# Attention scores as one fp16 product of 96 stacked rows per head, with query and key halves carried through DRAM, and the stages from the scores on one iteration later

## What is computed

```
x = x + tanh(g_xattn) * attention(layernorm(x), ctx, ctx)      # B=2, S=2048, E=512, T=128 keys, 16 heads of 32
    q = (query @ Wq.T + bq), k = (key @ Wk.T + bk), v = (value @ Wv.T + bv)   split into heads
    att = q k^T / sqrt(32); masked by pad_mask and subsq_mask; prob = softmax(att); out = prob v
x = x + tanh(g_ffn) * ffn(layernorm(x))
    shared_out = (silu(x sg) * (x su)) sd
    top 2 of softmax(x router), 8 experts: routed = sum of coef * ((silu(x gate) * (x up)) down)
```

## Time and profile before

| | us |
|---|---|
| median of 3 runs | 1158.11 (1152.9 to 1160.1) |
| the profiled execution, its own time | 1157.58 |
| its span in the trace | 1155.8 |
| pass 1 up to the end of iteration 12 on DVE | 180.71 |
| iterations 13 to 31 (19 iterations) | 270.04 |

### The profile page before, as it was taken

The page is one execution under the profiler, slowest core; times in us unless marked ns, Lnnn a source line. Parts: engine busy times, 40 slices in busy tenths (PEclk is TensorE's granted clock), DMA queues, the critical chain, the costliest instruction groups (busy, mean ns, idle before and its releaser), DMA issues.

```text
span 1155.8 us, 26617 instructions
## 1 busy us (share of the span) xinstructions
PE 1050.2 (91%) x7344; PEld 677.3 (59%) x7345; DVE 822.7 (71%) x2938; ACT 531.4 (46%) x1041; POOL 441.8 (38%) x654
## 2 busy tenths in 40 slices
PE   4699979999999999860899999999999999999997
PEld 3488767777777777660455555555554444444443
DVE  5899868788888888763576666666665666666666
ACT  1366546666666666640444444444443232232322
POOL 3254647676667667442112112112110423232322
PEclk9999889999999999855899999999999999999999
DMA  7555573223323223432233333333332544444543
GB/s 290 197 177 179 131 173 95 93 93 93 93 93 94 94 93 110 101 102 72 74 110 118 115 113 118 118 109 118 118 109 67 185 158 161 157 168 149 169 149 128
DMA packets 76731, 146.96 MB, mean 127 GB/s; under 512 B 20912, under 2 KB 23088, under 8 KB 73872
## 3 DMA queue, kind: packets, MB, share of 16 engines
q1 hardware_dynamic: 46512, 66.01, 20.0%
q10 hardware_dynamic: 17280, 44.83, 10.5%
q0 software_dynamic: 12896, 35.58, 9.9%
HBM read 94.04 MB, written 52.35 MB: 127 GB/s over the span
## 4 chain that ended last, share of the span: by engine, by line
PE 64%; issue 11%; DVE 9%; POOL 8%; ACT 4%; DMA 2%; POOLq 1%; another core or an unknown queue 1%; SPq 0%; DVEq 0%; ACTq 0%
PE bank L1046 15%; PE bank L1047 15%; PE bank L1048 15%; PE bank L1038 8%; PE bank L1090 3%; PE bank L1108 3%; DVE arena L776 3%; POOL arena L467 3%; POOL token_of_row L503 2%; ACT arena L605 1%; DVE arena L865 1%; POOL arena L474 1%; DMA token_of_row<-arena 1%; DVE peak L879 1%; PE bank L1064 1%
## 5 line engine op out<-in xcount | busy, mean ns | idle before, releaser
L1046 PE MATMUL bank<-weights,arena 128*128 (+1 forms) x682 | 259.9, 381 | 2.1 <-ACT arena L647 1.9
L1047 PE MATMUL bank<-weights,arena 128*128 (+1 forms) x682 | 259.8, 381 | 0.0
L1048 PE MATMUL bank<-weights,arena 128*128 (+1 forms) x682 | 259.6, 381 | 0.0
L1038 PE MATMUL bank<-ident,arena 128*128 128x128 f32 (+1 forms) x1592 | 189.4, 267 | 56.1 <-DMA arena<-normed_rows,arena 25.7
L1038 PEld LDWEIGHTS bank<-ident,arena 128*128 128x128 f32 (+1 forms) x1592 | 161.4, 132 | 103.0 <-issue 71.9
L514 POOL DMA_INDIRECT arena<-normed_rows,arena x71 | 67.1, 946 | 254.9 <-PE bank L1038 238.7
L1108 PEld LDWEIGHTS bank<-arena 128*128 128x128 f32 x1024 | 131.7, 198 | 34.3 <-issue 29.5
L1090 PE MATMUL bank<-arena 128*128 128x512 f32 x256 | 138.8, 647 | 5.4 <-DVE arena L776 5.1
L1108 PE MATMUL bank<-arena 128*128 128x33 f32 x1024 | 128.8, 276 | 2.9 <-issue 1.8
L467 POOL TENSOR_TENSOR arena<-arena 128x512 f32<-128x512 f32 x96 | 101.3, 1056 | 76.8 <-DVE arena L776 75.7
L524 POOL DMA_INDIRECT arena<-expert_rows,arena x64 | 62.8, 981 | 173.9 <-DVE arena L998 156.1
(11 more groups left out here) (175 smaller groups left out, 1895.7 us busy)
## 6 DMA issues: line engine op xcount, KB each, us to landing
expert_rows<-arena ACTq DMA_DIRECT2D x71, 256.0 KB, 2.1
arena<-in_x SPq DMA_DIRECT2D x64, 256.0 KB, 3.2
weights<-in_w_gu ACTq DMA_DIRECT2D x8, 1024.0 KB, 4.7
x_rows<-arena SPq DMA_DIRECT2D x32, 256.0 KB
normed_rows<-arena SPq DMA_DIRECT2D x32, 256.0 KB, 4.9
normed_transposed<-arena SPq DMA_DIRECT2D x32, 256.0 KB, 2.3
arena<-normed_transposed SPq DMA_DIRECT2D x32, 256.0 KB, 3.3
arena<-x_rows SPq DMA_DIRECT2D x32, 256.0 KB, 3.4
```

The lines of the kernel that those rows point to most:

```text
L1038: last = t.transpose(dst[:, c * P:(c + 1) * P], src[:, c * P:(c + 1) * P], (ident16 if src.dtype == F16 else ident)[:, :])
L1046: t.matmul(dst, hi[:, rows], w_hi(c), start=(c == 0), stop=False)
L1047: t.matmul(dst, hi[:, rows], w_lo(c), start=False, stop=False)
L1048: last = t.matmul(dst, lo[:, rows], w_hi(c), start=False, stop=(c == chunks - 1))
```

## The change

1. The scores. Before, one fp32 product per group of four heads: 128 rows of `q_t` by 128x512 of `kbd`. Now, q is scaled, split in two fp16 halves and stacked on 96 partitions per head (upper, lower, upper), against keys stacked (upper, lower, upper of the array `k_halves`), so that one fp16 product of 96 rows by 128 columns gives a head's scores; four such products per group (`scores(k)`, L1144 of the new kernel).
2. The halves are moved across partitions through DRAM: SP writes `q_halves` to `q_dram` (one DMA), waits for its landing, and reads it back into `q_stack` in three DMAs of 32 partitions each (`stack`). The keys go the same way once (`k_dram`).
3. The copy of the queries out of `bank[0]`: ACT's four pieces of `q_t` become one fp16 copy at the end of its body (q_hi), and DVE gets a new step at the start of its next body, the lower half (q_lo). The query bias is now one more small product of PE per 128 columns (L1179 of the new kernel, `bq_half` and `bias_row`); the scale of the scores is applied by ACT's exponential.
4. The scores and all behind them have a lag one higher: LAG1 is 9, and there are 41 iterations.
5. PE's transposition of the normalised tile, first in its body before, stands behind `mix_values(0)`. ACT's x_hi, first in its body before, stands behind `exponent(0)`. DVE's x_lo, before `maxima(0)` until now, stands behind `maxima(1)`.
6. SP's body has a new order, with the q write first and the stack loads behind the loads of x.
7. Before the first scores: the peak of the keys and a scale for them (a third use of the peaks' transposition, `turn_peaks(7, 2)`), and three steps of POOL for the bias; the `memset` of `kbd` and the sixteen writes into it are gone. In passes 2 and 3 several semaphores are merged into one that counts on; their steps and their order are the same.

```diff
-        LAG1, LAG2, LAG3, SPAN2 = 8, 4, 4, 4
+        LAG1, LAG2, LAG3, SPAN2 = 9, 4, 4, 4
...
 SP body
+                n, j, u = tile(J, v, 3)
+                if live(n, NT):
+                    hold(sp, sp_passed, (q_ready, n + 1))
+                    sp.dma_start(q_dram[u].rearrange("a p n -> p a n"), q_halves.rearrange("p (a n) -> p a n", a=2)).then_inc(q_out[u], 16)
...
+                    hold(sp, sp_passed, (q_out[u], 16 * (j + 1)))
+                    hold(sp, sp_passed, (s_done, group(n - 2, EC - 1)))
+                    stack(q_stack[u], q_dram[u], q_stacked[u])
...
+            def stack(dst, src, done):
+
+                for at, part in enumerate((0, 1, 0)):
+                    sp.dma_start(dst[at * D:(at + 1) * D, :].rearrange("d (h n) -> d h n", h=HG),
+                                 src[part].rearrange("(h d) n -> d h n", h=HG)).then_inc(done, 16)
...
 ACT body
-                    act.wait_ge(xt_done, n + 1)
-                    need(act, q_done, n)
-                    a.activation(x_hi, bank[0][:, :], ACT.Copy, scale=X_SCALE).then_inc(hi_ready, 1)
...
                 take_probs(0)
                 take_probs(1)
                 exponent(0)
+                n, j, u = tile(J, v, 2)
+                if live(n, NT):
+                    act.wait_ge(xt_done, n + 1)
+                    need(act, q_done, n)
+                    a.activation(x_hi, bank[0][:, :], ACT.Copy, scale=X_SCALE).then_inc(hi_ready, 1)
...
-                    for c in range(EC):
-                        last = a.activation(q_t[u][:, c * P:(c + 1) * P], bank[0][:, c * P:(c + 1) * P], ACT.Identity,
-                                            scale=w_back[:, 0:1], bias=bq_s[:, c:c + 1])
-                    last.then_inc(q_ready, 1)
+                    hold(act, act_passed, (q_out[(v - 3) % 2], 16 * (j + u)))
+                    a.activation(q_halves[:, 0:E], bank[0][:, :], ACT.Copy, scale=Q_DOWN).then_inc(q_hi_ready, 1)
...
 DVE body
+                n, j, u = tile(J, v, 3)
+                if live(n, NT):
+                    dve.wait_ge(q_hi_ready, n + 1)
+                    d.scalar_tensor_tensor(q_halves[:, E:2 * E], bank[0][:, :], Q_DOWN, q_halves[:, 0:E], ALU.mult, ALU.subtract).then_inc(q_ready, 1)
...
-                n, j, u = tile(J, v, 2)
-                if live(n, NT):
-                    dve.wait_ge(hi_ready, n + 1)
-                    d.scalar_tensor_tensor(x_lo, bank[0][:, :], X_SCALE, x_hi, ALU.mult, ALU.subtract).then_inc(lo_ready, 1)
                 maxima(0)
...
                 maxima(1)
-                normalise(1, 5)
+                n, j, u = tile(J, v, 2)
+                if live(n, NT):
+                    dve.wait_ge(hi_ready, n + 1)
+                    d.scalar_tensor_tensor(x_lo, bank[0][:, :], X_SCALE, x_hi, ALU.mult, ALU.subtract).then_inc(lo_ready, 1)
+                normalise(1, 6)
...
 PE body
-                    transposes(bank[0], xn[u], EC).then_inc(xt_done, 1)
-
                 def scores(k):
-                    n, j, u = tile(J, v, 3)
+                    n, j, u = tile(J, v, 4)
                     if live(n, NT):
-                        pe.wait_ge(q_ready, n + 1)
+                        pe.wait_ge(q_stacked[u], 16 * PARTS * (j + 1))
+                        pe.wait_ge(k_stacked, 16 * PARTS)
                         need(pe, max_done, group(n, k - 2))
-                        t.matmul(bank[2 + k % 2][:, :], q_t[u][:, k * P:(k + 1) * P], kbd[:, u, k, :],
-                                 start=True, stop=True).then_inc(s_done, 1)
+                        for h in range(HG):
+                            q_at, k_at = (h * EC + k) * P, ((h * EC + k) * B + u) * T
+                            last = t.matmul(bank[2 + k % 2][:, h * T:(h + 1) * T], q_stack[u][0:STACK, q_at:q_at + P],
+                                            k_stack[0:STACK, k_at:k_at + T], start=True, stop=True)
+                        last.then_inc(s_done, 1)
...
+                            last = t.matmul(dst, bq_half[:, co * P:(co + 1) * P], bias_row[:, :], start=False, stop=True)
...
                 mix_values(0)
+                n, j, u = tile(J, v, 2)
+                if live(n, NT):
+                    pe.wait_ge(xn_ready, n + 1)
+                    need(pe, q_ready, n)
+                    transposes(bank[0], xn[u], EC).then_inc(xt_done, 1)
                 scores(2)
```

More of the change, by code:

```diff
@@ L150, in build @@
         x_hi, x_lo = carve(E // 2).bitcast(F16), carve(E // 2).bitcast(F16)
-        q_t = [carve(E) for _ in range(2)]
+        q_halves = carve(E).bitcast(F16)
+        q_stack = [carve(H * T // 2).bitcast(F16) for _ in range(2)]
         attn = carve(E)
@@ L597, in body @@
                         sc = score[u][:, h * T:(h + 1) * T]
-                        last = a.activation(sc, sc, ACT.Exp, bias=peaks_neg[:, h - H + HG:h - H + HG + 1])
+                        last = a.activation(sc, sc, ACT.Exp, scale=score_scale[:, :], bias=peaks_neg[:, h - H + HG:h - H + HG + 1])
                     last.then_inc(exp_done, 1)
```

292 lines of the change are left out of this document (166 added, 126 removed).

## The result

The changed kernel takes 1229.35 us, the median of 4 runs (1226.53 to 1233.14), against 1159.11 us (1152.9 to 1162.04, 4 runs): a ratio of 1.0617, interval 1.0578 to 1.0656. The direction and the mechanism were forecast, the size was not: 1199 was said, and 1226 was the end of the range. The profiled execution took 1233.14 us, its span 1231.3, which is 75.5 more than before.

A forecast was written before the change was run, and what follows sets the result against it. Pass 1 was taken to stand on two close limits, PE and a ring through POOL. Terms 20.8 + 10 + 7 + 3 = 41 us on 1157.6 gave 1198.4, about 1199 against the median; range 1162 to 1226.

The forecast's parts named there:

- What bounds the kernel now: Pass 1, 14.21 us per iteration: odd iterations set by PE and mendable, even ones by a 14.3 us loop through POOL.
- The moved x_hi and x_lo: Steady iterations 13 to 31: DVE's second half waits for POOL and ACT, 16.2 us even, 14.5 odd, +20.8 us.
- PE's work: Pass 1 scores: PE's iteration falls from 12.7 to about 10.0 us, but this brings no gain since PE waits.
- The start: Before the first scores: PE's first transposition waits for a longer chain of peaks and DVE steps, +3 us (1 to 5).
- The q path through DRAM: SP's query write and three reads per iteration: about 10 us at most, hidden within 14 us, so 0 us.
- One more iteration: Pass 1 runs 41 iterations instead of 40: +10 us, between about 9 and 14.5.
- the other iterations with scores: About ten iterations before 12 and in the drain: 0 to 1.5 us each, 0.7 taken, +7 us.
- The signs: Expected in the loop's profile: L881 idle about 3 us each, shift(0) never idle before, scores near 1 us, PE at most 75%.
- The waits did not vanish: Rival for the loop: POOL's stretch from L873 to shift(0) shrinks, so DVE's waits vanish; 1137 to 1152 us, chance 0.16.
- Start and drain were not free: Rival: the steady loop loses as forecast, but start and drain cost nothing; 1165 to 1180 us, chance 0.10.
- The lower clock: Rival: PE idles into its lower clock, 1 to 2 us more per iteration, 1217 to 1237; with late q path, chance 0.08.
- the ring: Steady loop: L873, POOL's scatter, shift(0), exponential, x_hi, x_lo, back to L873; 16.2 us even, 14.5 odd, 15.35 on average.

The follow-up runs named there:

- k6: Kernel before, each fp32 score product replaced by four fp16 products of 96 rows on constant weights, nothing else changed: 1153.43 us, ratio 0.9979.
- c3: Kernel before with POOL's scatter moved one iteration later, behind the second norm's scale: 1145.28 us, ratio 0.9878.
- k1: Changed kernel with ACT's x_hi moved back ahead of the exponential of group 0: 1193.47 us, ratio 1.0336.
- k34: Changed kernel with ACT's L654 behind iteration 1's weight loads and SP's key write, wait and stack one iteration later: 1220.94 us, ratio 1.0375.
- k5: Changed kernel without the query write and stack loads from tile 2 on (later scores not the reference's): 1210.76 us, ratio 1.0455.
- c1: Changed kernel with x_hi ahead of exponential 0, iteration 1's weight loads before L654, key transfers one iteration later, reloads spread over three iterations: 1174.37 us, ratio 1.0141.
- c0: The changed kernel measured once more, unchanged, on another chip: 1228.43 us, ratio 1.0623 to the kernel before.

## Why the prediction went wrong, by its own steps

*What bounds the kernel now*: right for the even iterations. PE was busy 252.6 of 270.0 us in the loop and not what set the time. k6 gave PE its shorter product and moved the kernel by 0.2%; c3 took 1.3 us out of POOL's stretch, 1.1 out of the even iteration, and moved it by 1.2%. That the odd iterations are PE's, and that the change can mend them, k6 does not bear out for their usual length, 13.56 us, which stayed. The iteration of 14.88 us that stood in the earlier trace rows was one of the longer ones.

*The moved x_hi and x_lo*, +20.8 us: right in mechanism and size. Forecast 16.2 and 14.5 us, measured 16.03 and 14.69; forecast 290.8 us for 19 iterations, measured 294.1. Two even iterations of 17.2 and 17.5 us stand 2.7 us above the others, and the rest is the odd ones' 0.2 us each, less what the even ones stay under the forecast. k1 undoes this term alone, and the loop falls by 31 us.

*PE's work*: its price per product was right. L1144's starts are 0.055 us apart at the full clock (407.690 to 407.745) and 0.107 at the lower one (185.833 to 185.940). Its busy time is 50.9 us for 512 products, 1.6 us an iteration instead of 0.9 for the same sixteen, since they come in groups of eight, four and four, each with its last product's 0.22 us at the end, and in part at the lower clock: eight take 0.61 us from start to end at the full clock and 1.04 at the lower one. It changed nothing, since PE waits.

*The start*, +3 us, bounds 1 to 5: **the step that failed first.** It measured 20 us in iteration 2, of which iteration 3 gave 4 back (9.1 us for 13.0). The sum counted the peaks' transposition and six small DVE steps, which are there and take, with the two additions to the values ahead of them, 3.1 us (32.52 to 35.63). It left out what the scale holds up: ACT's weight loads behind L654, and SP's load of x behind a landing in DRAM. I named the queue for the queries' path and not for the keys', where it costs most. k34 brings back 12 us by the end of iteration 3.

*The q path through DRAM, 0 us*: **the step that failed second**, and only beside the reload. "The stores of x1 and of the normed tiles, which nobody waits for within the iteration" is wrong as a cost of nothing: DVE's L864 waits for one of them in its next body, and in iteration 11 the path had pushed the store behind the reload. "About 10 us at most" for the path's own five issues is wrong there too: PE waited until 185.65 for loads issued from 164.28 on, and the next write took 17.6 us until SP could go on. In the 19 steady iterations the path costs nothing (k5: 292.8 for 294.1 us), in iteration 11 16 to 17 us, in iterations 10 to 12 together 16.5 (k5: 47.7 for 64.2). The prediction kept an excess of 2 us per iteration for the range; it had no term for a single large stall.

*One more iteration*, +10, and *the other iterations with scores*, +7: together about right, in part by the way of counting. The drain is 13.8 us longer, and what is left before the loop, once iterations 2, 3 and 11 are taken out, is 37.3 - 20.0 + 4.0 - 17.0 = 4.3 us (with 0.8 us of it ahead of iteration 2). Together 18 for 17. With iterations 10 to 12 taken as one, 11.9 us, it is 23 for 17. No run has the extra iteration alone.

With what was measured the sum reads: loop 24.1, iterations 2 and 3 together 16, iteration 11 17.0, the rest of pass 1 18.1, passes 2 and 3 0.3, that is 75.5, the difference of the spans. The forecast had 20.8 + 3 + 0 + 17 + 0.

*The signs.* L881 waited for L617 in all 19 iterations, 2.3 us each and 43.6 in all, for about 3 and 60. `shift(0)` had no idle time before it, in odd iterations too. The scores' line took 1.5 us per iteration in the loop, not 1. PE was busy 89% of the loop, not at most 75%: that sign left out what the lower clock adds.

*The rivals.* The waits did not vanish: POOL's stretch stayed at 6.3 us. Start and drain were not free: they lost 37.3 and 13.8 us. The lower clock came: the granted clock in the loop fell from 0.97 to 0.85, and PE's busy share from 94% to 89%. The Trainium skill's rule of "TensorE: Matmul & The Clock Gate", section "What's actually happening", that activity releases the throttle, points the same way. But it did not set the end: the even iterations take 16.03 us at a granted clock of 0.79 (420.00 to 436.03) and 16.04 at 1.00 (358.57 to 374.61). The time landed above 1216 by other causes: the ring and the start. The forecast's 0.08 there was for the lower clock "or a late q path", and of the latter iteration 11 had 17 us once, not 1 to 2 in every iteration.

The query write landed fast in the steady loop: in 18 of the loop's 19 iterations SP went on 2.4 or 2.5 us after its issue, and 2.8 us in the other. The estimate by the Trainium skill, "DMA: Bandwidth & Descriptors", section "Anatomy of one DMA — SWDGE (gpsimd) path", was 2.6 us; that section is about DMAs issued by GpSimd, and these are issued by SP. Beside other transfers the same write took 7.08 us at iteration 10 and 17.6 in iteration 11, and the keys' write 6.91, above the rows' 4.9 us as well.

## What to carry to other kernels

A wait put in the middle of a strictly ordered DMA queue must be costed by everything queued behind it, one by one, with the question of who waits for each and what large transfer it will then run beside; the steady loop can hide it all, while the first iterations and the one with a bulk load pay. When a step is moved behind a wait, close the ring through all engines: four durations and one sum gave the loop here within 1.1%. PE, busy 94% of the loop but not on that ring, gave almost nothing back when its work was cut; the 1.2% that could be had lay in the order of POOL, at 38% the least busy engine of the kernel.

## What was not expected of the hardware

Work removed from PE shows in its busy time only in part. In k6, the only change is a shorter product, and the granted clock in the loop went from 0.97 to 0.85; PE's busy time fell by 11 us for the 50 that left its score line. It is no fixed price: with the same short products and the new bias products the granted clock was 0.95 in k1 (PE busy 238.25 of 262.90 us) and 0.89 in c1, whose loop has the same code (250.8 of 268.2).

A 256 KB store took 20.08 us from issue to landing when three loads of 1 MB had been issued up to 2 us ahead of it on another engine's queue; the loads themselves landed after 7.6, 18.3 and 20.2 us. A 256 KB load took 10.74 us behind two such loads. Issued 0.2 us ahead of the three, the store held DVE for 3.3 us instead of 16.4 (c0).

A step of POOL on one column, L542, takes 1.70 us beside DVE's weight split L969 (1.74 in the earlier trace rows), and in c3, where it has moved past that neighbour, 0.27 us. There the scatter meets it instead, and its second DMA takes 2.60 us on POOL where 0.96 is usual: the delay goes to whatever runs beside the split. The one-column step ends 0.13 us after the split in the changed kernel and 0.14 in the kernel before, as if it had waited for the split's end.
